# Log decay gates in two f32r parts, and the low part of the activations made later

## The reference

```python
xn = layernorm(x)                              # over the last axis, eps 1e-5
# attention part: 16 heads, key size 16, value size 32
q, k = split(xn @ qk_w.T); v, g_out = split(xn @ vg_w.T)
q, k, v = (silu(causal_dwconv(a, w, 4 taps)) for a, w in ...)
beta = 2 * sigmoid(xn @ b_w.T + b_bias + beta_bias)
g = -exp(A_log) * softplus(xn @ a_w.T + dt_bias)      # log decay, per step and head
q = l2norm(q) * 16 ** -0.5; k = l2norm(k)
for t:                                          # state S (16 x 32) of each head
    S = S * exp(g_t)
    S = S + outer(k_t, (v_t - k_t @ S) * beta_t)
    o_t = q_t @ S
o = o * rsqrt(mean(o * o) + eps) * silu(g_out)
attn = o @ o_w.T
# feed-forward part, weights of 4 bits with a scale per 128 inputs
h = silu(xn @ w_gate.T) * (xn @ w_up.T)         # 1408 wide
y = h @ w_down.T; ffn = y / sqrt(mean(y * y) + 1e-6)
out = x + attn + ffn
```

## Time and profile before

| | |
|---|---|
| median of three runs | 3350.01 us |
| the profiled execution, its own time | 3347.2 us |
| its span, first to last instruction | 3345.4 us |
| mean granted TensorE clock | 0.988 |
| PE busy | 3174.2 us, 95% of the span |
| PE weight loads busy | 2253.2 us, 67% |
| DVE busy | 2429.0 us, 73% |
| ACT busy | 1664.4 us, 50% |
| POOL busy | 1840.9 us, 55% |

### The profile page before, as it was taken

The page is one execution under the profiler, slowest core; times in us unless marked ns, Lnnn a source line. Parts: engine busy times, 40 slices in busy tenths (PEclk is TensorE's granted clock), DMA queues, the critical chain, the costliest instruction groups (busy, mean ns, idle before and its releaser), DMA issues.

```text
span 3345.4 us, 118358 instructions
## 1 busy us (share of the span) xinstructions
PE 3174.2 (95%) x45632; PEld 2253.2 (67%) x45632; DVE 2429.0 (73%) x5407; ACT 1664.4 (50%) x3306; POOL 1840.9 (55%) x2737
## 2 busy tenths in 40 slices
PE   5999999999999999999999999999999999999995
PEld 4666766766666766666666667666667666666664
DVE  7677777777777777777777777777777777777772
ACT  3444554545554445545445545445545455544452
POOL 3565455665455664456654456654556654466543
PEclk8999999999999999999999999999999999999996
DMA  3111111111111111111111111111111111111111
GB/s 111 39 46 27 37 43 33 45 39 27 40 40 39 46 33 30 43 34 45 46 27 37 43 33 46 45 26 35 43 36 46 36 28 43 37 42 46 27 31 30
DMA packets 318316, 132.07 MB, mean 39 GB/s; under 512 B 277088, under 2 KB 278880, under 8 KB 317792
## 3 DMA queue, kind: packets, MB, share of 16 engines
q1 hardware_dynamic: 313824, 119.26, 14.2%
q10 hardware_dynamic: 4096, 6.42, 0.6%
HBM read 75.30 MB, written 50.33 MB: 38 GB/s over the span
## 4 chain that ended last, share of the span: by engine, by line
PE 63%; DVE 13%; POOL 8%; issue 8%; ACT 4%; DMA 2%; SPq 1%; ACTq 1%; DVEq 1%; POOLq 0%
PE PS L1148 14%; PE PS L1216 7%; PE PS L1135 7%; PE PS L1104 6%; PE PS L1136 6%; PE PS L1357 5%; DVE arena L876 4%; POOL arena L499 4%; POOL work L495 3%; PE PS L1281 3%; PE PS L1202 3%; DVE inner L978 2%; PE PS L1234 2%; DVE arena L373 2%; PE PS L1252 2%
## 5 line engine op out<-in xcount | busy, mean ns | idle before, releaser
L876 DVE SCALAR_TENSOR_TENSOR arena<-PS,sc,arena 128x256 f32<-128x256 f32 x2112 | 1004.3, 482 | 294.0 <-ACT arena L596 193.6
L1135 PE MATMUL PS<-xh,wgu 128*128 128x256 f32 x2816 | 871.5, 341 | 36.0 <-DVE arena L876 35.5
L596 ACT ACTIVATE arena<-PS,sc 128x256 f32<-128x256 f32 x704 | 330.7, 475 | 759.6 <-PE PS L1136 703.6
L1136 PE MATMUL PS<-xl,wgu 128*128 128x256 f32 x2816 | 698.8, 281 | 0.0
L1148 PE MATMUL PS<-wdn,inner 128*128 128x512 f32 x1408 | 650.7, 592 | 0.0
L1135 PEld LDWEIGHTS PS<-xh,wgu 128*128 128x128 f32 x2816 | 531.2, 189 | 156.1 <-issue 85.2
L495 POOL TENSOR_TENSOR work<-arena 128x31 f32<-128x31 f32 (+15 forms) x992 | 511.4, 516 | 138.4 <-DMA arena<-scr_a 63.2
L499 POOL TENSOR_TENSOR arena<-arena,work 128x31 f32<-128x31 f32 (+15 forms) x992 | 543.7, 548 | 77.8
L1136 PEld LDWEIGHTS PS<-xl,wgu 128*128 128x128 f32 x2816 | 530.3, 188 | 83.2 <-issue 83.2
L1104 PE MATMUL PS<-xnT,wqkv 128*128 128x256 f32 x2048 | 498.7, 392 | 27.4 <-ACT inner L576 19.6
L1104 PEld LDWEIGHTS PS<-xnT,wqkv 128*128 128x128 f32 x2048 | 384.5, 194 | 107.5 <-ACT inner L576 33.2
(11 more groups left out here) (141 smaller groups left out, 4553.8 us busy)
## 6 DMA issues: line engine op xcount, KB each, us to landing
xt<-in_x SPq DMA_DIRECT2D x64, 256.0 KB, 2.8
scr_a<-arena SPq DMA_DIRECT2D x64, 256.0 KB, 2.4
arena<-scr_a SPq DMA_DIRECT2D x256, 64.0 KB, 3.2
obuf<-in_x SPq DMA_DIRECT2D x64, 256.0 KB, 2.8
scr_t<-arena SPq DMA_DIRECT2D x32, 512.0 KB, 2.7
arena<-scr_t SPq DMA_DIRECT2D x256, 64.0 KB, 2.3
out<-obuf SPq DMA_DIRECT2D x64, 256.0 KB, 2.0
wqkv<-in_wqkv ACTq DMA_DIRECT2D x1, 2048.0 KB, 12.9
```

Of the source, the lines that this page charges most:

```text
L596: eng.activation(fa[:, u % 4, :], PS[:, bank(u, 0), 0:NB * P], ACT.Copy, scale=sc[:, u % 2, KB * m:KB * m + 1]).then_inc(fa_scaled.sem, 1)
L876: eng.scalar_tensor_tensor(out=fa[:, u % 4, :], in0=PS[:, bank(u, k // 2), k % 2 * NB * P:][:, 0:NB * P], scalar=sc[:, u % 2, KB * m + k:K ...
L1135: eng.matmul(o, w, xh[:, k, :], start=True, stop=False)
L1136: ins = eng.matmul(o, w, xl[:, k, :], start=False, stop=True)
```

## The change

The gates g are split by POOL into gh, rounded to f32r, and gl = g - gh. `masked_g` makes gm from gh (now an f32r tensor) and a second masked tensor `gml` from gl, which lies in the memory of xl. `log_decay` runs two f32r products, `laterR` with gm and `laterR` with gml, in place of one float32 product. The exponential E moves to another place in the arena, so gm now waits for the product of the tile before and not for its reader on DVE. The subtraction that makes xl leaves `split_x`, becomes `rest_of_x`, and stands behind `layer_norm_scale` in POOL's queue; it also waits for `log_decay`, since gml has its memory. DVE gets one copy more at the start, which makes laterR.

```diff
+        gml = xl[:, :, :].rearrange("p k t -> p (k t)").rearrange("p (b h i) -> p b h i", b=NB, h=H)
+        E = arena[:, 9216:10240].rearrange("p (b h i) -> p b h i", b=NB, h=H)
...
             eng.tensor_copy(xh[:, :, :], xnT[:, :, :]).then_inc(xh_done.sem, 1)
+
+        def rest_of_x(eng, n):
+
             hold(eng, *xh_done.at(n, 1))
+            hold(eng, *decay_out.at(n, NB))
             eng.tensor_tensor(xl[:, :, :], xnT[:, :, :], xh[:, :, :].bitcast(F32), ALU.subtract).then_inc(xl_done.sem, 1)
 
         def masked_g(eng, t, n):
-            if t:
-                hold(eng, *p_done.at(t, NB))
-            for b in range(NB):
-                eng.tensor_tensor(gm[:, b, :, :], g[:, b, :].unsqueeze(2).broadcast_to([P, H, CH]),
-                                  tri[:, :].unsqueeze(1).broadcast_to([P, H, CH]), ALU.mult).then_inc(gm_done.sem, 1)
+
+            hold(eng, *g_done.at(n, 1))
+            eng.tensor_copy(gh[:, :, :], g[:, :, :]).then_inc(g_split.sem, 1)
+            hold(eng, *g_split.at(n, 1))
+            eng.tensor_tensor(gl[:, :, :], g[:, :, :], gh[:, :, :].bitcast(F32), ALU.subtract).then_inc(g_split.sem, 1)
+            hold(eng, *g_split.at(n, 2))
+            for part, dst in ((gh, gm), (gl, gml)):
+                if part is gh and t:
+                    hold(eng, *decay_out.at(t, NB))
+                for b in range(NB):
+                    eng.tensor_tensor(dst[:, b, :, :], part[:, b, :].bitcast(F32).unsqueeze(2).broadcast_to([P, H, CH]),
+                                      tri[:, :].unsqueeze(1).broadcast_to([P, H, CH]), ALU.mult).then_inc(gm_done.sem, 1)
...
                 if more:
                     layer_norm_scale(eng, n.next())
+                rest_of_x(eng, n)
                 next_tile(eng, t, n)
...
+            eng.tensor_copy(laterR[:, :], later[:, :]).then_inc(consts_done.sem, 1)
...
-                eng.wait_ge(*gm_done.at(n, b + 1))
+                eng.wait_ge(*gm_done.at(n, NB + b + 1))
                 eng.wait_ge(*cin_done.at(n, NQKV - 1 + b))
-                eng.matmul(PS[:, 4 + b, :], later[:, :], gm[:, b, :, :].rearrange("p h i -> p (h i)"), start=True,
-                           stop=False)
+                for part in (gm, gml):
+                    eng.matmul(PS[:, 4 + b, :], laterR[:, :], part[:, b, :, :].rearrange("p h i -> p (h i)"),
+                               start=(part is gm), stop=False)
```

More of the change, by code:

```diff
@@ L117, in build @@
         negm = sb("negm", [P, CH], BF16)
+        laterR = sb("laterR", [P, P], F32R)
         identb = sb("identb", [P, P], BF16)
@@ L157, in build @@
         work = sb("work", [P, C // 2])
-        gm = sb("gm", [P, NB, H, CH])
-        E = gm
+        gm = sb("gm", [P, NB, H, CH], F32R)
         gx = sb("gx", [P, NB, H * DK])
@@ L178, in build @@
         g = sb("g", [P, NB, H])
+        gh = sb("gh", [P, NB, H], F32R)
+        gl = sb("gl", [P, NB, H], F32R)
         bet = sb("bet", [P, NB, H])
@@ L205, in build @@
         t_read = signal("t_read", 128)
-        gm_done = signal("gm_done", 2)
+        g_split = signal("g_split", 2)
+        gm_done = signal("gm_done", 4)
         gx_done = signal("gx_done", 2)
@@ L1179, in decay_sums @@
                     eng.wait_ge(consts_loaded.sem, 16 * 11)
-                    eng.wait_ge(consts_done.sem, 6)
+                    eng.wait_ge(consts_done.sem, 7)
                 sums = PS[:, 6, 0:NB * (2 * H + NHALF * NC)].rearrange("p (b n) -> p b n", b=NB)
```

## The result

The changed kernel took 3332.19 us (median of five runs, 3329.68 to 3334.45), the kernel before 3350.68 (3347.69 to 3353.64) beside it: ratio 0.9946, 95% interval [0.9935, 0.9957]. The profiled run took 3332.51 us with a span of 3330.7. The forecast was 3344 with a range of 3335 to 3364. It is faster, as the likeliest case had it (but that case had 0.39 against 0.38 for no change), by three times as much as forecast, and outside the range.

The account below looks back on a forecast made before the run. PE, with 63% of the chain, and its waits were taken to bound the kernel. Terms -6.5 - 2.0 - 1.0 + 2.0 + 1.0 + 0.2 = -6.3 us, from median 3350.0 to 3344 us; range 3335 to 3364.

Parts of the forecast that it names:

- the likeliest case: Whole kernel: the forecast of 3344 us itself, chance 0.62, of which 0.31 faster, 0.29 same, 0.02 slower.
- The log decay's saving: Both log decay blocks: 0.48 us each, 31 us of PE work, lost waiting at `turn_kqn(0)`; counted 0.
- The first rival: Log decay: its saving on PE arrives after all, giving 3313 us; chance 0.08.
- xl leaves the tile's front: a small gain: Tile front: the halo copy stops waiting for POOL, PE's wait ahead of `project(4)` goes; -6.5 us in the loop.
- The second tile: Front of the second tile: the halo copy is alone on the path, so -2.0 of its 6.40 us wait.
- The first tile: First tile: one convolution instruction of 2493 ns taken as waiting for xl; -1.0 us, between -2.0 and 0.
- The split on POOL: POOL's gh, gl and two more masks, 3.2 us, hidden with 7 us to spare before PE; 0.
- The third rival: `conv(2)`: the extra masks hold its instructions, ending it 1.4 us later per tile; 3386 us at worst, chance 0.10.
- the ratio 4.32 to 2.71: `conv(2)` beside gx and gm against `conv(4)` with POOL idle, in us; would also fit mere slowing by 1.6.
- The new place: xl behind the root: DVE's `state(3)` 1.63 us late, mostly absorbed by 1.69 slack before `gram(1)`; +2.0 us.
- The second rival: `state(3)`: DVE's wait for xl exceeds the slack, PE 0.7 us late at `gram(1)` every tile; 3363 us, chance 0.20.
- The last tile: Last tile: with no next layer norm, xl meets `state(1)`, for which `y_times_s(2)` waits; +1.0 us, between 0 and 1.63.

Follow-up runs that it names:

- first, again, third: Unedited repeats of both kernels: before 3350.68, changed 3332.19 us; then before 3350.0 us, changed at ratio 0.9943; then before 3348.5, changed 3330.3 us.

## Why the prediction was wrong

Three traces of each kernel (first, again, third) give each term as a mean of starts; the mean spans are 3344.9 and 3330.2 us, -14.6 by the unrounded spans:

- **The log decay's saving, 0 forecast: right.** 166.7 to 166.8 us in the sixteen traces in which `turn_kqn(0)` kept its place. The wait is now in two places, in the median tile 0.38 us by starts inside `y_times_s(1)` and 0.38 between `k_times_u(1)` and `turn_kqn(0)`; together they take what the two blocks save, 0.40 and 0.38. The saving per block was forecast at 0.48. The first rival, 3313, fell.
- **"xl leaves the tile's front: a small gain", -6.5 in the loop: the step that failed.** The mechanism was right (copy at 0.18 us, PE's wait for L576 gone), the size was not: 278.2 to 264.0 us over 30 tiles, **-14.2**. I had taken the recorded idle, 0.19 to 0.2 a tile, for PE's lateness, which was 0.46. The trace of before had the number in its starts; the 0.27 us that were missed, 30 times, are the 8 us between the two. xl moved alone has the same front (279.3 us over 31 tiles, 279.1 in the changed kernel), so the f32r passes have no part in it.
- **The second tile, -2.0:** its front from 17.9 to 15.7, -2.2. **The first tile, -1.0:** its start to the next one's 103.6 to 102.6, -1.0.
- **The split on POOL, 0: right.** gml ends at 1662.59, 7.5 us before PE reads it, and `conv(2)` is 0.6 us shorter, not longer. The third rival fell: a mask does hold one instruction of `conv(2)`, as it supposed, but the masks of gl start behind the last one. The single rows also settle what the ratio 4.32 to 2.71 left open: two instructions were held and four were not, so it was no even slowing by 1.6.
- **The new place, +2.0:** `gram(0)` to `gram(1)` 102.3 to 103.4, **+1.1** (in the first pair 0.6, where the idle record of that wait grew by 4.8, from 23.9 to 28.7); DVE was 1.56 late, where 1.63 was forecast. The trace agrees with the Trainium skill, SBUF — State Buffer, "Who interferes with whom", that VectorE with two inputs in SBUF and GpSimd reading SBUF shut each other out: the pair took 2.04 us where 0.48 stood and ended at 1686.54, right behind xl (1686.26); mere slowing would have added 0.9. The second rival fell, but the small margin was real: on the 3336 us chip, where PE pauses less of itself, the new place costs 5.6 us instead of 1.1.
- **The last tile, +1.0:** its start to the end 166.2 to 168.5, +2.3. **Startup, +0.2:** +0.5, with 22.3 to 25.2 us over all traces.

The sum of these is -14.2 - 2.2 - 1.0 + 1.1 + 2.3 + 0.5 = -13.5, with the 0.4 that the last tile's front gained counted twice, so -13.1. The other 1.5 of the 14.6 are what is left of stretches in which nothing was changed, single ones of which differ by up to 2.5 us either way. The medians differ by 18.1 to 18.5: the profiled runs of before lie on average 2.7 us under their medians and those of the changed kernel 0.9 over them, so carrying a sum over profiled runs to a median was off by another 3 to 4 us, which the range did not allow for. With -14.2 in its place the forecast would have been 3336: of the 12 us between 3344 and the measured 3332, 8 are the front, and the other 4 are mostly this step.

## What to carry to other kernels

Read how late an engine with pipelined instructions comes from start to start against an unbroken stretch of the same instructions; the idle records miss what the modelled ends and the restart behind a pause cover, and 0.27 us in each of 30 tiles was more than the whole forecast gain. A small copy on VectorE that takes ten times its usual length points at a GpSimd instruction beside it: look for a stretch in which VectorE waits for someone else, and put that instruction there. Shortening PE's work ahead of a wait that another engine's chain sets gave nothing in that stretch. Here the two edits of one change gave 14 to 16 us and 5 to 6 us when each was made alone, and the second no more than 2.5 on top of the first; only runs of each alone could tell.

## What was not expected of the hardware

- TensorE pauses for 0.12 to 0.6 us with nothing to wait for, among the 32x32 products, at places that hop from tile to tile. `p_times_u(2)` to unit 1 has a median of 1.00 to 1.24 us a tile in the kernels on the chips that take about 3349 us and 0.83 to 0.85 in the eight that ran where before takes 3336. That may be part of the 14 us between chips; no trace of before itself was had there. Whether the supply of instructions makes them was not tried.
- They cover other waits. With xl behind the root, `gram(0)` to `gram(1)` is 0.7 to 1.6 us longer in all on the chips with the long pauses and 4.5 to 5.6 on the one with the short ones: a VectorE that comes later is hardly seen at `gram(1)` where PE comes late there of itself.
- Behind an f32r pass of 512 columns the next matmul starts after 0.23 to 0.24 us (0.31 to 0.34 for the first of a block), behind the float32 product after 0.96.
